# First attention on one Trainium2 core: the weighted sums leave PSUM by VectorE instead of ScalarE, and all turned query tiles leave it by ScalarE

## What is computed

```python
# x: 32 x 128 x 256, ctx: the same shape, mask: 32 x 128 x 128
def _mha(q, k, v, mask):
    scores = jnp.einsum('bhqd,bhkd->bhqk', qh, kh) / jnp.sqrt(jnp.float32(hd))
    scores = scores + mask[:, None, :, :].astype(scores.dtype) * NEG_INF
    probs = jax.nn.softmax(scores, axis=-1)
    out = jnp.einsum('bhqk,bhkd->bhqd', probs, vh)
...
x = x + _L0_xattn_ref(_layernorm(x, axis=-1), ctx_1024, ctx_1024, mask_BxSxS2_ik1)
x = x + _L0_ffn_ref(_layernorm(x, axis=-1), L0_ffn_w_gate, L0_ffn_w_up, L0_ffn_w_down)
...
```

## Time and profile before

| what | value |
|---|---|
| median of three runs | 1371.85 us |
| the profiled execution's own time | 1375.09 us |
| its span | 1373.3 us |
| busy shares of the span | PE 95%, PEld 83%, DVE 81%, ACT 75%, POOL 29% |
| mean granted TensorE clock | 0.985 of full speed |
| first stage | from 0 to about 242 us |
| one step inside its hardware loop | 6.60 us |
| busy in 139 to 192 us of the loop (53 us) | PE 50.2, DVE 48.4, ACT 46.9, POOL 29.9 us |

### The profile page before, as it was taken

The page is one execution under the profiler, slowest core; times in us unless marked ns, Lnnn a source line. Parts: engine busy times, 40 slices in busy tenths (PEclk is TensorE's granted clock), DMA queues, the critical chain, the costliest instruction groups (busy, mean ns, idle before and its releaser), DMA issues. The chain is left out here.

```text
span 1373.3 us, 34398 instructions
## 1 busy us (share of the span) xinstructions
PE 1304.2 (95%) x11246; PEld 1135.3 (83%) x11246; DVE 1112.4 (81%) x1998; ACT 1034.2 (75%) x2690; POOL 391.9 (29%) x676
## 2 busy tenths in 40 slices
PE   5999999999999999999999999999999689999998
PEld 2666666778887778899899999999998589999998
DVE  6889996879858889487687877878778768888887
ACT  3988887566579877763888888888887268888886
POOL 5555553000011110004122222222222134444443
PEclk9999999999999999999999999999999789999999
DMA  8411162475178999656123333243420375111110
GB/s 265 130 39 46 49 212 85 134 271 209 47 225 263 294 287 293 244 176 224 37 92 113 104 125 113 86 143 101 150 101 17 122 299 208 51 49 44 55 50 14
DMA packets 103253, 191.12 MB, mean 139 GB/s; under 512 B 12226, under 2 KB 67549, under 8 KB 98528
## 3 DMA queue, kind: packets, MB, share of 16 engines
q1 hardware_dynamic: 92480, 155.93, 33.6%
q0 software_dynamic: 10464, 33.57, 8.4%
q10 hardware_dynamic: 192, 0.13, 0.0%
HBM read 124.30 MB, written 68.03 MB: 140 GB/s over the span
## 5 line engine op out<-in xcount | busy, mean ns | idle before, releaser
L2375 ACT ACTIVATE c_w_raw<-c_ps_score,c_neg_max 128x128 f32<-128x128 f32 x512 | 181.9, 392 | 35.2 <-DVE c_neg_max L2168 27.5
L2724 PE MATMUL d_ps_hT<-d_zT,d_w_tile 128*128 128x128 f32 x1248 | 148.1, 278 | 1.3 <-DVE d_zT L2835 1.3
L2724 PEld LDWEIGHTS d_ps_hT<-d_zT,d_w_tile 128*128 128x128 f32 x1248 | 144.9, 194 | 2.1 <-DVE d_zT L2835 2.1
L2913 ACT ACTIVATE d_h<-d_ps_hT,d_b1T 128x128 f32<-128x128 f32 x312 | 88.6, 366 | 44.9 <-PE d_ps_hT L2724 44.9
L2375 ACT ACTIVATION_READ_ACCUMULATOR c_w_raw<-c_ps_score,c_neg_max 128x1 f32 x512 | 118.5, 232 | 0.0
L2737 PE MATMUL d_ps_y<-d_w_parts,d_hT 128*128 128x256 f32 x912 | 118.5, 286 | 0.0
L2737 PEld LDWEIGHTS d_ps_y<-d_w_parts,d_hT 128*128 128x128 f32 x912 | 111.6, 191 | 0.0
L2855 DVE TENSOR_TENSOR d_w_parts<-d_w,d_w_parts 128x1024 fp32r<-128x1024 f32 x76 | 92.9, 1222 | 21.7 <-ACT d_w_parts L2928 21.5
L2009 PE MATMUL c_ps_proj<-c_xnT,ahead_wq 128*128 128x256 f32 x768 | 107.1, 289 | 0.0
L2048 PE MATMUL c_ps_aux<-ahead_wo_high,c_attnT 128*128 128x256 f32 x512 | 101.9, 292 | 1.8 <-DVE logits L2192 1.8
L2009 PEld LDWEIGHTS c_ps_proj<-c_xnT,ahead_wq 128*128 128x128 f32 x768 | 95.1, 189 | 5.1 <-issue 5.0
(11 more groups left out here) (346 smaller groups left out, 3662.6 us busy)
## 6 DMA issues: line engine op xcount, KB each, us to landing
keys_scratch<-b_out SPq DMA_DIRECT2D x64, 256.0 KB, 4.8
values_scratch<-b_out SPq DMA_DIRECT2D x64, 256.0 KB, 4.7
ahead_kT<-keys_scratch SPq DMA_DIRECT2D x16, 1024.0 KB, 6.1
d_w<-w_in SPq DMA_DIRECT2D x16, 1024.0 KB, 7.6
split_scratch<-b_split SPq DMA_DIRECT2D x12, 1024.0 KB, 5.1
c_v_more<-values_scratch SPq DMA_DIRECT2D x24, 512.0 KB, 4.0
a_w<-w_in SPq DMA_DIRECT2D x16, 512.0 KB, 6.5
b_ctx_high<-split_scratch POOLq DMA_DIRECT2D x16, 512.0 KB, 5.1
```

What stands on the lines that cost most here:

```text
L2375: last = act.activation(prob[:, n, j, :], ps_score[:, n % 2, j, :], ACT.Exp, bias=neg_max[:, n, j:j + 1], accum_out=row_sum[:, n, j:j + 1])
L2724: last = pe.matmul(ps_hT[:, f, :], w1_tile[:, half, k, n * P:(n + 1) * P], zT[:, s, k, :], start=(k == 0), stop=(k == ND - 1))
L2913: act.activation(h[:, f, :], ps_hT[:, f, :], ACT.Relu, bias=b1T[:, e, f:f + 1]).then_inc(h_ready, 1)
```

## The change

VectorE gets `copy_out` and loses its half of `copy_qy`; ScalarE loses `copy_out` and copies `qT` and `yT` in every step. VectorE's order inside a step becomes: both maxima, the copy of the weighted sums, the subtraction, then the statistics of batch b-3, the reciprocal of batch b-2, the aggregate of batch b-3. `normalise` and `largest` stay where they were. TensorE's, GpSimd's and SyncE's instructions and their order are unchanged.

```diff
+                def copy_out(b):
+                    dve.wait_ge(out_done, NQ * (b + 1))
+                    if inside(b, 1, NB - 1):
+                        dve.wait_ge(out_turned, b)
+                    dve.tensor_copy(outT[:], ps_out[:].rearrange("p (q k) -> p q k", k=P)).then_inc(outT_ready, 1)
...
-                def copy_qy(g, s):
-                    dve.wait_ge(qy_done, g + 1)
...
                     if here:
                         maximum(b, 0)
+                    if here:
+                        maximum(b, 1)
+                    if inside(b, 2, NB + 1):
+                        copy_out(b - 2)
+                    if here:
+                        subtract(b, s)
                     if last:
                         deviation(b - 3, 1 - s)
-                    if here:
-                        maximum(b, 1)
+                    if inside(b, 2, NB + 1):
+                        invert(b - 2, s)
                     if last:
                         aggregate(b - 3, 1 - s)
-                    if here:
-                        subtract(b, s)
-                    if s == 1:
-                        copy_qy(b + 2, s)
-                    if inside(b, 2, NB + 1):
-                        invert(b - 2, s)
                     if ahead:
                         statistics_ahead(b, u)
...
                     if here:
                         shifted_exponentials(b, u % 2, 0)
-                    if inside(b, 2, NB + 1):
-                        copy_out(b - 2)
-                    if here:
                         shifted_exponentials(b, u % 2, 1)
                         exponentials(b, u % 2)
-                    if u % 2 == 0:
-                        copy_qy(b + 2, 0)
+                    copy_qy(b + 2, u % 2)
```

More of the change, by code:

```diff
@@ L677, in copy_qy @@
                         act.activation(yT[:, :, bass.ds((g - 6) * P, P)], ps_qy[:, 1], ACT.Copy).then_inc(yT_ready, 1)
[L679 to L683, removed]
                 def step(b, u):
```

## The result

The changed kernel takes 1384.01 us (median of four runs, 1381.66 to 1385.65), the kernel before 1371.16 us (median of four runs, 1367.42 to 1372.67). The ratio is 1.0101, 95% interval 1.0086 to 1.0116: slower by 1.0% (12.9 us between the medians). I had forecast 1372.2 us and no change, with a range up to 1380. The time lies outside it.

What follows compares the result with a forecast made beforehand. VectorE was to bound the first stage at 6.59 us a step against 6.60: 31 steps give -0.3 us, the stage's end +0.6, so +0.3; forecast median 1372.2 us, range 1366 to 1380.

Steps and rivals of the forecast that it cites:

- VectorE's own step, summed: First stage's loop: VectorE's instructions and one stall add to 6.55 us a step, up to 6.63; 6.59 taken.
- The rest: `normalise` 0.32: Last part of VectorE's step: `normalise` 0.32 us, ahead aggregate 0.23, `largest` 0.34.
- The copy, 0.68 us: VectorE's copy of the weighted sums out of PSUM takes 0.68 us, costing 0.60 of a step.
- rival (A): VectorE copies the weighted sums at the SBUF rate; its sum is 6.28 us, the kernel 1362.5 us; chance 0.04.
- The stall ahead of `normalise`, 0.32 us: In each step VectorE idles 0.32 us for GpSimd's inverse deviation; aggregate to `normalise` takes 1.12 us.
- VectorE becomes the bound, its wait for the scores goes: In the first stage's loop VectorE has no idle time except one stall; its loop lies at the old period.
- The end of the stage, +0.6 us: Last steps: batch 30's late inverse deviation delays batch 31's residual 0.5 us; +0.6 us in all, ends 0 and 1.2.
- (C): VectorE's instructions lose their overlap around waits: 6.84 us a step, 1379.9 us; chance 0.13.
- The chain through ScalarE, 6.38 us: Transposes, weighted sums, copy, subtraction, ScalarE's second half and first probability copy take 6.38 us, hidden by VectorE's 6.55.

Runs made afterwards that it cites:

- the run with the narrow residual: Changed kernel, but GpSimd's residual adds only one column of the attention to x instead of 256: 1370.51 us, ratio 0.9995 to the kernel before.
- with constants: Changed kernel, but `normalise` subtracts and multiplies by constants instead of the mean and inverse deviation read from SBUF: 1376.75 us, ratio 1.0047 to the kernel before.
- with the turned tiles: Copy swap alone, statistics as before, with ScalarE copying `qT` and `yT` between its second and third copies of turned probabilities: 1360.87 us, ratio 0.9935 to the kernel before.

## Why the prediction was wrong

**The step that failed** is one term of "VectorE's own step, summed": "The rest: `normalise` 0.32". It measured 0.83 in the step shown (145.66 to 146.49), 0.51 more, because in the new order the instruction falls on GpSimd's residual. VectorE's loop is closed, so all of that is in the period: the changed kernel's steps are 7.06 us on average and those of the run with the narrow residual 6.60, 0.46 apart. The prediction looked at GpSimd only as the one who delivers the inverse deviation. It did not ask what GpSimd does next. The answer stood in its own paragraph on the end of the stage: the residual is queued behind the inverse deviation. When that is late, its end releases both: `normalise` on VectorE, and on GpSimd the residual, whose own wait (the division) is over by then. Moving the aggregate back did not only show a stall of 0.3 us, it made two instructions that share something start within 0.07 us of each other, in 31 of 32 batches. Before, the division released the residual while `normalise` was already running (161.34 against 161.07). A sign of it lay in the prediction's own: the residual there takes 0.83 us, and 0.73 in the loop.

The Trainium skill has the rule that I left out: "SBUF — State Buffer", section "Who interferes with whom", says that GpSimd's only pair of SBUF ports is VectorE's second pair, that a VectorE instruction in a two-port mode takes it for its whole length, and that whoever issues first blocks the other. The traces above agree: `normalise` 0.41 alone and 0.80 to 0.91 behind the residual, the reduction undisturbed, and with constants both outcomes. Who came first is not always who has the earlier record, as the near ties above show. That ports are the thing shared is the page's account; the runs show the exclusion, not its place, and no run shows directly in which mode `normalise` runs. An estimate from the rows: the 0.15 us that are left of it once the residual is over are too few for 256 columns at the 1.05 ns of the rows that read PSUM (0.27 us), so with its operands too it moves them at the faster rate.

Point by point:

- **The copy, 0.68 us**: right, 681 ns, 32 times. The fast copy, rival (A), did not happen.
- **The stall ahead of `normalise`, 0.32 us**: right. The interval from aggregate to `normalise` was forecast as 1.12, with 1.20 as its other end; it measures 1.12 in two steps of four (144.54 to 145.66) and 1.21 in the other two (137.52 to 138.73). In the latter `normalise` starts behind the residual and the next instruction follows 0.74 us later instead of 0.83, so both kinds come to 1.95 us, where the prediction had 1.44 to 1.52.
- **VectorE becomes the bound, its wait for the scores goes**: right. The sum without the collision, 6.59, measured 6.60 in the run with the narrow residual. One thing in it was not foreseen: the loop's turn costs 0.2 us once in four steps, made up by steps of 6.50.
- **The end of the stage, +0.6 us**: from the last batch's first maxima (231.03) to 252.88 it is 21.85 us, before 242.63 - 221.19 = 21.44: +0.4. About right.
- **The first steps**: not in the prediction. The third step starts 1.7 us earlier than before (29.31 against 30.98). The stretches of lower granted clock lie elsewhere, 0.88 from 24 to 28 us and 0.70 from 28 to 32 before, 0.50 from 20 to 24, 0.81 from 24 to 28 and 1.00 from 28 to 32 after; what part of the 1.7 us is theirs, no run shows. From there to the last step the new kernel loses 11.5 us in 29 steps, 0.40 a step.
- **The parts together**: -1.7 + 11.5 + 0.4 is the 10.2 us of the trace. The medians differ by 12.9 (11.8 to 15.9 by the interval); in the profiled executions of this study the stages behind the first took 1126 to 1131 us whatever was changed (1126.4 with the narrow residual, 1130.9 in the changed kernel), and that scatter is what I put the rest down to, without a run that shows it.
- **The rival that ended on the slow side, (C)**, named the right engine and came nearest with 6.84 us a step (7.06 measured), but by another mechanism, lost overlap. That it lies close is luck: instructions still overlap, and the copy takes 0.60 from start to start.
- **The chain through ScalarE, 6.38 us**: about right. It shows when the statistics stay in place, as steps of 6.39 to 6.50, and it breaks when the copies of the turned tiles leave it.

## What to carry to other kernels

When a wait is moved so that one event releases instructions on VectorE and GpSimd together, write both of them down side by side and look whether either reads or writes SBUF tiles in a form that excludes the other; a duration taken from a trace in which they did not meet is not the duration when they do. A change made of two parts should be costed as two changes: here the swap of copies was worth a little, and the reordering lost about 10.6 us on the kernel before and 15 on top of the swap. And a chain that leaves an engine idle can take work that is not urgent into that wait: with the turned tiles this cost nothing and gave the largest gain of the study.

## What the runs showed of the hardware

- VectorE's `tensor_scalar` from SBUF to SBUF (128x256, f32) and GpSimd's addition of two SBUF tiles exclude each other: 0.41 becomes 0.80 to 0.91 us on VectorE if GpSimd has what they share first (0.71 if the residual started 0.16 us ahead); 0.72 becomes 0.83 to 0.85 us on GpSimd if VectorE has it first. The earlier record does not always win: with its one-column operands VectorE loses with a lead of 0.03 us and wins with one of 0.16; with constants it wins with one of 0.03. A GpSimd copy from SBUF to SBUF delays it too (0.60 us).
- A VectorE reduction over one SBUF tile of the same size beside the same GpSimd instruction kept its 0.38 to 0.42 us.
- The same `tensor_scalar` takes 0.41 us with two one-column operands from SBUF and 0.29 us with constants.
- The turn of VectorE's four-step hardware loop cost about 0.2 us in the changed kernel (7.2 against 7.0 us) and with constants (6.57 against 6.40), but nothing visible with `normalise` ahead of the division (6.68 to 6.78 throughout) or where TensorE sets the step (6.28).
